# A fill of eight columns, and a wait for it, ahead of every four gathers on GpSimd

## The reference, cut to what matters

```python
# layer 0: GATv2, twice; layer 3: the same form with 8 heads
xj = xl[src]
e = leaky_relu(xj + xr[dst], 0.2);  logits = e @ att
ex = exp(logits - segment_max(logits, dst)[dst])
out = segment_sum(ex / denom[dst] * xj, dst)      # denom = segment_sum(ex, dst)
# layer 1: attn = exp(leaky(p1[dst] + p2[src]));  agg = segment_sum(attn * emb[src], dst) / denom
#          (in the kernel this layer's indices run the other way and it scatters)
# layer 2: score = leaky(logit[dst] + logit_src[src]); softmax over dst; segment_sum(attn * nft[src], dst); GRU
```

## Time and profile before

| what | us |
|---|---|
| median of three runs | 14912.77 (14884.54 to 14926.11) |
| the profiled execution's own time | 14998.32 |
| its span | 14996.4 |
| busy: PE, DVE, ACT, POOL | 11026.0, 7973.5, 5541.4, 9489.8 |
| the four gather passes, from first to last gather | about 2630, 2632, 2609 and 2754 |
| the scatter pass, about | 3300 |

### The profile page before, as it was taken

One profiled execution on the slowest core, in us unless ns is written; L12 is line 12 of the kernel. 1 busy time (PEld: TensorE's weight loads), 2 busy tenths in 40 slices (PEclk: granted clock), 3 DMA queues, 4 the chain that ended last, 5 costly groups with the idle time before them and its releaser, 6 DMA issues.

```text
span 14996.4 us, 278163 instructions
## 1 busy us (share of the span) xinstructions
PE 11026.0 (74%) x60653; PEld 8678.6 (58%) x60653; DVE 7973.5 (53%) x29240; ACT 5541.4 (37%) x14105; POOL 9489.8 (63%) x8593
## 2 busy tenths in 40 slices
PE   5777777777777778888888875555555767777776
PEld 4666666666666666666666653344344556666664
DVE  6555555555555555555555553333333566666666
ACT  1444444344444444333333343333333622222223
POOL 3666666466666657888888865566666255655555
PEclk7887788788778775766666765555555877888777
DMA  3111111221111113444444452222222221222222
GB/s 87 45 45 44 44 45 45 88 80 44 45 44 45 44 40 44 39 39 39 39 39 39 39 104 58 44 45 45 45 45 45 60 52 48 50 49 49 50 50 56
DMA packets 808955, 748.01 MB, mean 50 GB/s; under 512 B 264685, under 2 KB 691174, under 8 KB 808254
## 3 DMA queue, kind: packets, MB, share of 16 engines
q0 software_dynamic: 453440, 550.05, 21.1%
q1 hardware_dynamic: 354814, 191.38, 4.9%
HBM read 548.62 MB, written 192.13 MB: 49 GB/s over the span
## 4 chain that ended last, share of the span: by engine, by line
PE 27%; another core or an unknown queue 15%; issue 13%; DMA 9%; DVE 7%; ACT 6%; POOL 2%; SPq 1%; DVEq 1%; ACTq 0%; POOLq 0%
DMA scatter_s<-dst_side 8%; PE bank L738 8%; PE bank L721 3%; PE bank L722 3%; PE bank L1214 3%; ACT oh_e L826 2%; PE bank L1220 2%; PE bank L1229 2%; PE bank L747 2%; PE bank L705 1%; POOL scatter_s L1181 1%; DVE agg L960 1%; DVE lrelu L915 1%; DVE agg L951 1%
## 5 line engine op out<-in xcount | busy, mean ns | idle before, releaser
L738 PE MATMUL bank<-rows,oh_e 128*128 128x130 f32 x9984 | 2172.6, 376 | 1578.7 <-ACT oh_e L826 1172.1
L1181 POOL DMA_INDIRECT scatter_s<-dst_side x1664 | 2568.6, 1544 | 551.9 <-DMA scatter_s<-dst_side 267.1
L738 PEld LDWEIGHTS bank<-rows,oh_e 128*128 128x128 f32 x9984 | 1804.0, 264 | 1918.7 <-issue 1036.4
L826 ACT ACTIVATE oh_e<-bank,weight,minus_w 128x128 f32<-128x128 f32 x4992 | 1880.3, 459 | 2378.4 <-remote 1620.8
L951 DVE SCALAR_TENSOR_TENSOR agg<-agg,rescale,bank 128x130 f32 x4992 | 1683.4, 337 | 1636.6 <-remote 792.6
L722 PE MATMUL bank<-rows,ident 128*128 128x128 f32 x9984 | 2335.9, 319 | 144.8 <-issue 141.1
L687 POOL DMA_INDIRECT rows<-gather_c,edge_sb x1664 | 1650.9, 992 | 1122.4 <-issue 443.9
L687 POOL DMA_INDIRECT rows<-gather_b,edge_sb x1664 | 1672.5, 1005 | 1061.9 <-issue 423.0
L687 POOL DMA_INDIRECT rows<-gather_a,edge_sb x1664 | 1669.1, 1003 | 1008.5 <-issue 412.0
L687 POOL DMA_INDIRECT rows<-gather_s,edge_sb x1664 | 1574.3, 946 | 1061.2 <-issue 443.2
L722 PEld LDWEIGHTS bank<-rows,ident 128*128 128x128 f32 x9984 | 1894.7, 235 | 159.7 <-issue 157.6
(11 more groups left out here) (352 smaller groups left out, 18169.2 us busy)
## 6 DMA issues: line engine op xcount, KB each, us to landing
rows<-gather_a,edge_sb POOLq DMA_INDIRECT x1664
rows<-gather_b,edge_sb POOLq DMA_INDIRECT x1664
scatter_s<-dst_side POOLq DMA_INDIRECT x1664
rows<-gather_s,edge_sb POOLq DMA_INDIRECT x1664
rows<-gather_c,edge_sb POOLq DMA_INDIRECT x1664
rows<-scatter_s SPq DMA_DIRECT2D x56, 455.0 KB, 6.3
scatter_s<-zeros SPq DMA_DIRECT2D x64, 390.0 KB
edge_sb<-edge_tab SPq DMA_DIRECT2D x520, 40.0 KB
```

The costliest lines, as they stand in the source:

```text
L738: ins = e.matmul(sum_bank(g)[:, (g % 2) * AW:(g % 2) * AW + L.aw], oh_e[:, g % 8, :], r, start=True, stop=True)
L826: e.activation(oh_e[:, g % 8, :], bank[7][:, (g % CH) * P:(g % CH + 1) * P], ACT.Relu, bias=weight[:, it.slot(2, 2), g:g + 1], scale=minus ...
L1181: e.indirect_dma_start(scatter_s[k], bass.IndirectOffsetOnAxis(ap=S_.target[:, it.slot(1), g:g + 1], axis=0), S_.summed[:, g % 8, :], None ...
```

## The change

A buffer `pause` of eight columns is added, and one semaphore for it. At the head of each chunk, behind the wait for a free buffer and in front of its four gathers, GpSimd fills the buffer with zeros and then waits for the fill's own semaphore. Nobody reads the buffer.

```diff
+        pause = sb("pause", [P, 8])
...
+                self.paused = four("pause_filled")
...
                 for c in range(NCH):
                     w.hold_ge(L.block.at(it, c, lag=U))
+                    e.memset(pause[:, :], 0.0).then_inc(L.paused.sem, 1)
+                    w.hold_ge(L.paused.at(it, c))
                     for g in range(c * CH, (c + 1) * CH):
                         w.hold_ge(L.side.at(it, g - LEAD) if g >= LEAD else L.side.at(it, g + G - LEAD, lag=1))
                         e.indirect_dma_start(rows[:, u, g, 0:L.width], None, L.src_rows,
```

## The result

Timed beside each other, the changed kernel took 14762.0 us (median of 4 runs) and the kernel before 14915.0: a ratio of 0.9901, 95% interval 0.9884 to 0.9918, so 1.0% less or 153 us. The forecast was 14662, 251 less. The profiled execution took 14754.5 us against 14998.3, 244 less. The forecast took its 251 us from that one long execution and carried them over to the median whole, so 153 is what it is to be measured by.

A forecast was written before the change was run, and what follows sets the result against it. It took the passes as bound by alternating gather bursts and standstills. POOL's floor of 10062 us plus remaining waits gave 10374 against 10625, 251 less; 14912.8 - 251 = 14662 us, 8-in-10 range 14350 to 15250.

The forecast's parts named there:

- Direction and range: Whole kernel: faster 0.52, same 0.12, slower 0.36; 14662 us, own range 14350 to 14860, 8 in 10 14350 to 15250.
- The mechanism: Gather passes: back-to-back gathers make PE's signals late; they arrive when POOL falls silent, so a rest can pay for itself.
- rival A: Gather passes: 1.2 us pauses too short, standstills stay, 252 of 1,664 pauses unabsorbed, costing 227 us: 15140; chance 0.28.
- The pause: POOL ahead of each chunk: 1.2 us in place of 0.30, +0.9 each, 1498 us in sum.
- Rival B: POOL's pauses: the fill's signal is held up too, gaps of 1.9 us, +601: 15514; chance 0.08.
- The waits that stay: Passes a, b, s, c: waits added to POOL's floor by judgement, 52, 52, 62 and 146 us.
- What covers it: POOL ahead of the gathers: 2257 us of waiting is more than the pauses' 1498.
- Rival C: Gather passes: long waits are PE's plain work, the pause eats into them, 14913 within 45 us; chance 0.12.
- my thaw: Gather passes: PE's held signals come all at once when POOL falls silent for one or two microseconds.
- The waits at PE: POOL's waits at PE in the gather passes: to fall from 2334 to some 300 us.
- the floor: POOL in the four passes, busy time plus gaps and pauses: 10062 us against 10625, gain at most 563.

The follow-up runs named there:

- fills: 21 fills ahead of each chunk, waiting only for the last fill of the chunk before, against the kernel before, in condition 1: ratio 0.9979.

## Why the prediction was right, point by point

**Direction and range** held, in condition 1, which is the one of the profile it was made from; of the 251 us forecast 153 came. **The mechanism** (bursts of gathers hold the others back, rests let them go on) is borne out by the times of PE's updates and by lead 16 with and without the pause. But it is a mechanism of condition 1, not of the kernel: in condition 2 gathers run back to back for 2077 us and nobody stands still. The prediction took what it read in one profile for a property of the program. For condition 2 it would have failed in direction: there rival A is the whole story, with all 1,664 pauses unabsorbed and not 252.

**The pause** was forecast at +0.9 us and is +0.77: 216 us less in all. The fill starts with no delay, for which 0.12 had been put in, and takes 122 ns; wait and restart together are 0.94, forecast 0.98. Rival B (1.9 us) is out: the fill's own signal isn't held up.

**The waits that stay** were judged at 52, 52, 62 and 146 us, 312 in all. Measured, each window less POOL's gathers, 1,248 x 0.30 and 416 x 1.07: in a 2581.8 - 1645.5 - 374.4 - 445.1 = 117, and in the same way 156 in b, 148 in s, 149 in c: 570. So this term was 258 too small, and the cheaper pause (216) with gathers 43 us shorter made it good. The sum of the passes came out to 2 us by errors that cancel, and by luck: the profiled execution before was 83 us longer than its median, so of the 253 us between the two profiles some 90 are probably no gain of the change.

**What covers it.** 2257 us of waits was 197 too many: 169.8 and 27.5 us of it (the earlier trace rows hold it, and the earlier trace rows leave those lines out) are waits for tables and the carry, mostly ahead of a pass's first gather, and can take in nothing. The waits within the passes are 10625 - 6567 - 1997 = 2061. If the pauses had only eaten into them, 2061 - 1281 = 780 would remain; 570 did. So of what the passes gained, 210 us are waits that vanished beyond that, and 43 are shorter gathers. Rival C (the pause eats into the waits) describes six sevenths of what happened to the waits, and my thaw the last seventh, which with the shorter gathers is the gain; less the 90 us it is smaller still.

**The waits at PE** were to fall from 2334 to 300; they fell to 1460. Part of that is the reading: a gather behind a pause whose last releaser is PE stands in this row with its whole 0.94 us. DVE's and ACT's waits at "remote" did not go either:

```profile
ACT oh_e L830 <- remote: 1542.2, 379, 9.9
...
DVE agg L955 <- remote: 964.1, 188, 9.9
...
DVE shifted L1072 <- remote: 734.5, 164, 8.1
```

Before, oh_e had 1620.8 us of such waits, agg 792.6, shifted 747.8 and rescale 905.1. Rescale's fell to 467.5, agg's rose. Lrelu's (ACT's L862) stayed, 784.7 and 769.7. The standstills became shorter and more: DVE's waits at "remote" went from 487 of 5.4 us on average to 568 of 4.1, and those over 8 us from 93 to 41. They didn't vanish, and the 4% that the floor allowed didn't come. The prediction had put down gaps of 1.2 us with DVE's long waits left as the sign of A, the slower outcome. The long waits were half left and the kernel was still faster, so this sign doesn't tell A from the forecast.

**What stays open.** What sets the condition: the chip itself (0 and 15 were quick, 14 and 5 slow), or something beside this core or of that hour; no chip was used twice, so no run parts them. Why PE's signals are held, and its issue is slow, while gathers go out, and why the scatters, 1544 ns each, don't do it. No run in condition 1 was without gathers; that they are what holds PE back rests on the stages without them in the same execution, on when the updates come, and on three changes of POOL's rhythm (lead 16, pause, fills). Lead 16 was not run in condition 2.

## What to carry to other kernels

Before a trick is built on a strange wait in a profile (idle engines with the releaser "remote", work that stands done before its reader starts), time the kernel again at another time and on another chip: here it took 14% less, the wait was gone, and the trick cost 11%. Where an engine is back to back, each gap on it is paid in full; where it has waits, most of a gap falls into them, and only what the gap frees elsewhere is gain. Only the change was timed in both conditions: it gains 153 us in one and loses 1418 in the other, so the kernel before is the one to keep.

## What the runs showed of the hardware

- One kernel, two conditions: 12,868 and 14,900 us. A gather's issue is 944 to 947 ns (median) in both, the granted clock 0.78 and 0.72 in the profiled runs of the kernel before, and the waits at "remote" are in the slow one alone. There half of PE's semaphore updates in the gather passes come more than 1 us late (5,757 of 11,589), in the quick one none of 13,155; 83% of the late ones come in idle times of GpSimd of 1 us and more.
- GpSimd starts a fill of 128x8 at once behind a gather, 122 ns; five take 0.27 us. A wait for its own result, written as in this loop, costs 0.77 us more than none.
- In condition 1 a lead of 16 in place of 10 costs 9.6%: more room for GpSimd to run ahead can make everything slower.
